# A graph network in one kernel: row loads of walk tables, the turn amid the products, scores ahead of the norm

## The reference

```python
edge_index = jnp.stack([src, dst])
h = jnp.maximum(_layernorm(x, axis=-1), 0.0)
x = x + _L0_gnn_ref(h, edge_index, ...)     # two SAGE convolutions, log softmax
h = jnp.maximum(_layernorm(x, axis=-1), 0.0)
x = x + _L1_gnn_ref(h, edge_index, ...)     # GAT, 4 heads of 128, batch norm, feed-forward
h = jnp.maximum(_layernorm(x, axis=-1), 0.0)
x = x + _L2_gnn_ref(h, edge_index, ...)     # GAT, 2 heads of 64, PReLU
h = jnp.maximum(_layernorm(x, axis=-1), 0.0)
x = x + _L3_gnn_ref(h, ..., src, dst, edge_type_4)  # max over edges, 4 relations
```

## Time and profile before

| | |
|---|---|
| three runs | 5915.43, 5924.08, 5924.83 us; median 5924.08 |
| the profiled execution | 5918.01 us, its span 5916.3 us |
| busy of the span | TensorE 3311.7 us (56%), VectorE 2935.2 (50%), ScalarE 1891.2 (32%), GpSimd 3914.0 (66%) |
| instructions | 100,213 |
| granted TensorE clock | 0.722 of full in the mean |

### The profile page before, as it was taken

One profiled execution on the slowest core, in us unless ns is written; L12 is line 12 of the kernel. 1 busy time (PEld: TensorE's weight loads), 2 busy tenths in 40 slices (PEclk: granted clock), 3 DMA queues, 4 the chain that ended last, 5 costly groups with the idle time before them and its releaser, 6 DMA issues. The chain is left out here.

```text
span 5916.3 us, 100213 instructions
## 1 busy us (share of the span) xinstructions
PE 3311.7 (56%) x15772; PEld 2786.6 (47%) x15773; DVE 2935.2 (50%) x7620; ACT 1891.2 (32%) x6493; POOL 3914.0 (66%) x4083
## 2 busy tenths in 40 slices
PE   3445555544565535889899894344555563333332
PEld 3444455444555524667777644233444533333331
DVE  4233344434455665788888744344555552222221
ACT  2111111111122204667777653233444441111110
POOL 4777777677777657777776005777777317777776
PEclk8666777766767757999999995566677785555555
DMA  4222222212122123444443211222222134444443
GB/s 122 61 62 63 64 65 66 71 52 53 52 53 53 48 47 87 109 115 116 115 111 106 99 38 38 54 53 53 53 53 53 25 105 131 131 130 132 133 131 108
DMA packets 441904, 474.75 MB, mean 80 GB/s; under 512 B 131954, under 2 KB 337214, under 8 KB 441695
## 3 DMA queue, kind: packets, MB, share of 16 engines
q0 software_dynamic: 130464, 264.37, 18.5%
q1 hardware_dynamic: 184116, 146.31, 8.2%
q10 hardware_dynamic: 127227, 63.09, 3.6%
HBM read 315.46 MB, written 157.97 MB: 80 GB/s over the span
## 5 line engine op out<-in xcount | busy, mean ns | idle before, releaser
L1175 PE MATMUL pa<-arena,weighted 128*128 x4480 | 871.3, 370 | 843.6 <-POOLq L893 510.2
L1175 PEld LDWEIGHTS pa<-arena,weighted 128*128 128x128 f32 x4480 | 803.8, 275 | 899.7 <-issue 899.4
L422 POOL DMA_INDIRECT arena<-y_tab,slot x784 | 739.7, 944 | 442.7 <-ACT slot L514 233.7
L1592 POOL DMA_INDIRECT arena<-t_tab,src_idx x784 | 788.1, 1005 | 283.2 <-issue 225.0
L899 POOL DMA_INDIRECT arena<-h_tab,src_idx x784 | 742.2, 947 | 307.3 <-issue 232.5
L2478 POOL DMA_INDIRECT arena<-t_tab,src_idx x784 | 751.1, 958 | 244.9 <-issue 232.5
L899 POOL DMA_INDIRECT arena<-sage_tab,src_idx x784 | 739.9, 944 | 261.3 <-issue 227.7
L471 DVE TENSOR_TENSOR_SCAN scan_t<-mask,scan_t,pa 128x512 f32<-128x512 bf16 x196 | 250.8, 1280 | 736.8 <-PE pa L495 736.8
L495 PE MATMUL pa<-ident,arena 128*128 128x128 f32 x784 | 218.5, 434 | 603.3 <-DMA arena<-y_tab,slot 603.3
L2716 PE MATMUL pa<-weighted 128*128 128x130 f32 x2240 | 440.2, 377 | 77.7 <-ACT weighted L2798 51.1
L495 PEld LDWEIGHTS pa<-ident,arena 128*128 128x128 f32 x784 | 140.4, 217 | 681.3 <-DMA arena<-y_tab,slot 428.2
(11 more groups left out here) (515 smaller groups left out, 6572.2 us busy)
## 6 DMA issues: line engine op xcount, KB each, us to landing
gat_tab<-out_rows SPq DMA_DIRECT2D x248, 260.0 KB
scan_rows<-out_rows ACTq DMA_DIRECT2D x196, 256.0 KB, 3.7
arena<-t_tab,src_idx POOLq DMA_INDIRECT x1568
mask<-cut_row SPq DMA_DIRECT2D x196, 128.0 KB, 3.1
arena<-h_tab,src_idx POOLq DMA_INDIRECT x784
arena<-sage_tab,src_idx POOLq DMA_INDIRECT x784
y_tab<-arena SPq DMA_DIRECT2D x49, 256.0 KB, 2.3
arena<-y_tab,slot POOLq DMA_INDIRECT x784, 2.8
```

The costliest lines, as they stand in the source:

```text
L422: nc.gpsimd.indirect_dma_start(out=rows(c, t), out_offset=None, in_=table[:, :], in_offset=bass.IndirectOffsetOnAxis(ap=slot[:, c, t:t + 1 ...
L1175: ins = nc.tensor.matmul(pa[:, b * CE:b * CE + RW], hot[b][:, t * P:(t + 1) * P], ring[:, bass.ds(start + t * RW, RW)], start=(t == 0), st ...
L1592: nc.gpsimd.indirect_dma_start(out=rows[:, g % QR * QT + t, :], out_offset=None, in_=t1_tab[:, :], in_offset=bass.IndirectOffsetOnAxis(ap= ...
```

## The change

A. `loaded_values` loads several values with one instruction and checks no bounds; `window_values` does it for a stretch of a window's row. The tables of a GAT are laid as one row for each window: 28 integers in `walk_rows1`, 24 in `walk_rows`. GAT1: ScalarE loads 16 registers (8 places in the ring, 8 offsets) and 10 registers (8 places, tile, groups needed) at the start of a window's body, VectorE 3 and 8. GAT2: ScalarE 8 at the start and 6 ahead of `stage_window`, VectorE 12 at the start and 3 ahead of `run`. In the walk passes TensorE's two loads for a step are one of two registers. `lay_walks` of GAT2 has four more copies and one more memset.

B. In `project` with `by_tile`, TensorE's turn and ScalarE's keep of group i+1 stand before the fifth tile of group i, not before its first, and the products of tiles go round four banks of PSUM instead of two.

C. In `project` with `starts`, VectorE waits for product i and does post i before front i+2.

```diff
+            banks = (pb[:, 0:CE], pb[:, CE:2 * CE], pd[:, 0:CE], pd[:, CE:2 * CE])
...
                     def step(i, b, left):
-                        if left > 1:
+                        if left > 1 and starts is None:
                             front(dve, i + 2)
                         dve.wait_ge(group_product.sem, group_product.past(i + 1))
                         post(dve, i, b)
+                        if left > 1 and starts is not None:
+                            front(dve, i + 2)
...
                         for t in range(NG):
                             if by_tile is not None:
+                                if t == 4 and left > 0:
+                                    turn(i + 1)
                                 ws, bias, n, _ = by_tile
 
-                                pe.wait_ge(tile_out.sem, tile_out.by_last_lap(i * NG + (t + 1 if t > 1 else 2 - t)))
-                                to = pb[:, t % 2 * CE:t % 2 * CE + n]
+                                pe.wait_ge(tile_out.sem, tile_out.by_last_lap(i * NG + (max(t, 1) if t < 3 else max(t - 1, 2))))
+                                to = banks[t % 4][:, 0:n]
...
-                        if left > 0:
+                        if left > 0 and by_tile is None:
                             turn(i + 1)
...
-                        if left > 0:
+                        if left > 0 and by_tile is None:
                             keep(i + 1, 1 - b)
                         if by_tile is not None:
                             for t in range(NG):
+                                if t == 4 and left > 0:
+                                    keep(i + 1, 1 - b)
                                 if t == NG - 2 and left > 1:
                                     scalar_front(act, i + 2)
                                 copy_product(i, t)
...
+        def loaded_values(kind, at, bounds):
+
+            why = "the walk tables are made on the chip from counts below these bounds"
+            _, values = nc.values_load_multi_w_load_instructions(at, engines=(kind,), skip_runtime_bounds_check_because=why)
+            return [nc.s_assert_within(value, low, high, skip_runtime_bounds_check_because=why)
+                    for value, (low, high) in zip(values, bounds)]
+
+        def window_values(kind, table, w, first, bounds):
+
+            last = first + len(bounds)
+            at = table[0:1, w, first:last] if isinstance(w, int) else table[0:1, bass.ds(w, 1), first:last].rearrange("o w k -> o (w k)")
+            return loaded_values(kind, at, bounds)
...
-                        start = pe.value_load(at[:, :, 0:1].rearrange("o s k -> o (s k)"), min_val=0, max_val=(RG - 1) * GT * RW)
-                        need = pe.value_load(at[:, :, 1:2].rearrange("o s k -> o (s k)"), min_val=1, max_val=GN)
+                        start, need = loaded_values(mybir.EngineType.PE, at.rearrange("o s k -> o (s k)"), [(0, (RG - 1) * GT * RW), (1, GN)])
...
-                        tile = of_fine(dve, w + 1, QW, 0, ET)
+                        tile, _, back = window_values(mybir.EngineType.DVE, walk_rows1, w + 1, 3 * QW, AHEAD1)
+                    if here:
+                        starts = window_values(mybir.EngineType.DVE, walk_rows1, w, 0, STEP1)
...
+                    if here:
+                        steps = window_values(mybir.EngineType.Activation, walk_rows1, w, 0, STEP1 + PLACE1)
+                    if next_here:
+                        *rows, tile, need = window_values(mybir.EngineType.Activation, walk_rows1, w + 1, 2 * QW, STEP1 + AHEAD1[0:2])
...
+                        values = window_values(mybir.EngineType.DVE, walk_rows, w, 0, STEP2 + PLACE2 + BLOCK2)
...
-                    need = of_walk(act, w, WT + 1, 1, GN)
-                    tile = of_walk(act, w, WT, 0, ET)
+                    *rows, tile, need = window_values(mybir.EngineType.Activation, walk_rows, w, 3 * WT, STEP2 + AHEAD2[0:2])
...
                     for k in range(WT):
-                        start = of_walk(act, w, k, 0, (RB - 1) * GT * BW)
...
                     if here:
-                        weigh(w, 0)
-                        weigh(w, 1)
+                        at = window_values(mybir.EngineType.Activation, walk_rows, w, 0, STEP2 + PLACE2)
+                        weigh(w, 0, at[0], at[WT])
+                        weigh(w, 1, at[1], at[WT + 1])
```

More of the change, by code:

```diff
@@ L1793, in run, with link @@
                                          run1[:, P - 1:P], ALU.add, ALU.max).then_inc(window_run.sem, 1)
-                def link(w, step, tile):
-                    back = of_fine(dve, w, QW + 2, 0, QK)
+                def link(w, step, tile, back):
                     v.tensor_copy(here1, tile_row1[:, :, bass.ds(tile, QK)])
@@ L1855, in body @@
                             if q == 4:
-                                link(w + 1, steps, tile)
+                                link(w + 1, steps, tile, back)
                             if q == 5:
@@ L1993, in _, with stage_flags @@
             def _(act):
-                def stage_flags(w):
-                    tile = of_fine(act, w, QW, 0, ET)
+                def stage_flags(w, tile, need):
                     after(act, window_scored, w)
@@ L2041, in body @@
                         if here:
-                            weigh(w, q, {t + 1: part for t, part in enumerate(beside)})
+                            weigh(w, q, steps[q], steps[QW + q], {t + 1: part for t, part in enumerate(beside)})
                         else:
@@ L2589, in run, with chain @@
                     v.tensor_tensor_scan(run_t, cut_t, own_row, -BIG, ALU.add, ALU.max).then_inc(window_run.sem, 1)
-                def chain(w, step, tile):
-                    back = of_walk(dve, w, WT + 2, 0, WK)
+                def chain(w, step, tile, back):
                     v.tensor_copy(tile_here, tile_row[:, :, bass.ds(tile, WK)])
```

130 lines of the change are left out of this document (61 added, 69 removed).

## The result

The changed kernel takes 5881.92 us in the median of four runs (5876.16 to 5883.32), the kernel before 5924.45; the ratio is 0.9927, with a 95% interval from 0.9916 to 0.9939. The profiled execution took 5876.16 us, its span is 5874.4 against 5916.3: 41.9 less. The forecast was 27.4 less on that span and 5893 for the median.

A forecast was written before the change was run, and what follows sets the result against it. GpSimd bounds the edge and walk passes and early windows; late GAT1 windows their own work, late GAT2 windows latencies. Terms 9.6 + 22 - 4 - 35 - 20 - 1 + 1 = -27.4 us on 5918.0 gave 5890.6, stated as 5893; range 5869 to 5907.

The forecast's parts named there:

- Project 1: First projection: scores before norm makes a 12.05 us chain per group, against 9.64 of scatter; +9.6 us, +8 to +11.
- Project 2: Second projection, norm on ScalarE: one chain of 14.4 us per group against 9.3; +22 us, range +17 to +25.
- The 80 in its list of signs: Expected sign in the second projection: scatters end 80 us after their first start instead of 65.
- the turn amid the products alone would be good: Second projection: this move alone helps, since the turn no longer waits for the norm ahead of all products; no size given.
- The rival that the two overlap in an unseen way: Projections lose nothing, since product and norm overlap in a way not seen; kernel at some 5853 us; chance 0.05.
- Project 3: Third projection: the first tile's product can start earlier, and half of the 8 us counts; -4 us, 0 to -8.
- Price of a read: Sequencer's row reads: 0.28 us for one register and 0.05 for each further one, 1.0 us for 16.
- rival A: Row reads: each register is its own trip; some 5960 us at 0.2 us each, 6015 at 0.275; chance 0.28.
- GAT1: Twenty late windows limited by their own work: 32.5 us each instead of 33.7; -20 us, range -10 to -30.
- GAT2: Late windows, a loop of latencies: 21.0 us each instead of 23.1 with fewer load delays; -35 us, -29 to -40.

The follow-up runs named there:

- projections alone: Kernel before with only the projections' edits (turn amid the products, four banks, scores ahead of the norm), all loads as before: 5952.24 us, ratio 1.0041.
- norm-first kernel: Changed kernel with the norm ahead of the scores again, turn amid the products and four banks kept: 5857.77 us, ratio 0.9881.
- row loads alone: Kernel before with the row loads, the function `project` as before: 5856.02 us, ratio 0.9880.
- The square above: Four kernels, reads single or in rows, checked or not; ratios to the kernel before (single, checked): single unchecked 0.9908, rows unchecked 0.9880, rows checked 1.0080.
- the moved reads: Kernel with the row loads alone, four reads moved behind work that might hide them: 7472.44 us (ratio 0.9699) and 7496.94 (0.9677), on slower chips.

## Why the prediction was right, point by point

**Project 1** held: +9.6 forecast, +8.9 here and +10.5 in the projections alone; copies 12.36 apart for 12.05. The copy, the product and the norm stand in one chain, and GpSimd waits 3.4 us a group where 2.4 were forecast: the seven scatters of a group take 9.0 us by themselves, and the 9.64 of the prediction was a mean in which the first three groups of before took 10.0 to 11.2.

**Project 2** held in its mechanism, every link with its size (7.8, 2.5, 0.9, 2.8, 0.3); 14.11 for 14.4 a group, GpSimd's wait of 5.4 as written. The 22 us became 18.3 because the scatters took 87.6 us from first to last, where the sum implies some 90 (first copy at 3588.7, scatter 0.9 behind it, end near 3680), and began 4.0 us sooner instead of 3. The 80 in its list of signs doesn't follow from its own sum. The norm-first kernel, which begins as early, shows that the sooner start comes from the turn amid the products. The prediction's remark that the turn amid the products alone would be good did not come true: it brings nothing in project 2's length (345.4 against 346.3). The rival that the two overlap in an unseen way (chance 0.05) is refuted by the projections alone.

**Project 3**: the step that failed is that half of the earlier start reaches the end. The start is 7 to 10 us earlier, the end isn't: 127.7 before, 127.4 with these edits alone, 127.7 with row loads and norm first. The 3.1 us less of the changed kernel are there in the row loads alone too (124.9) and are no larger than what this stage varies by with the same code (124.9 to 128.3), so the -4 is neither shown nor missed by its number.

**Price of a read** held where it carried the sum: 1.0, 0.8 and 0.6 us were taken for 16, 12 and 8 registers, 1.03, 0.85 and 0.56 are measured. For 10 (0.7 taken, 1.40 measured in most windows and 1.00 without other engines' reads beside it), 6 (0.5, 0.76), 3 and 2 it was too low. A single load has one assertion (L2451 has 240 of them for 240 reads) where the prediction counts two checks. So rival A, a trip for each register, is refuted, and with it what the Trainium skill's page "Runtime: NRT & Kernel Launch" (section "Instruction fetch mechanics") would give here: at its 200 ns per register sixteen would be 3.2 us, an estimate, and the trace has 1.03. The page speaks of loads from HBM; for a table in SBUF the trace disagrees for sixteen, and a read of two lies near 0.27 a register.

**GAT1**: the mechanism was right where it was priced. The prediction took the gain from the last twenty windows, 32.5 us each at their own pace and -20 in all; they have a median of 32.4, and together they are 21 us shorter. The other 9 of the 29.8 came before them, in the first ten windows, where the prediction had nothing. In the row loads alone the two parts are 22 and 2, with the norm first 18 and 4, so that this second part varies between kernels whose GAT1 differs by one check a row at most, and no run shows its cause.

**GAT2**: -35 forecast, -38.8 measured; the start of a window 0.5 us earlier on ScalarE and 0.9 on VectorE, where 0.6 was forecast for each, and the four staging copies within 0.52, where 0.25 apart was forecast. Of the 38.8, 32 came in the last twenty windows and 6 before them. The median window is 20.6 for 21.0, but the mean of the twenty is 21.5, because some still wait for gathers. So the near hit of the sum is in part luck: a little less than forecast in the windows that were priced, and a little more in those that were not.

**What the sum didn't say** is which part of a load cost the time. The prediction named both the checks and the reads and priced them as one. The square above shows that they don't simply add. Without the checks single loads already gain 54 of the 70 us and have the late windows of unchecked rows, and merging the reads brings the other 17. With the checks kept, merging the reads costs time (0.8% on its chip): there the checks stand together at the window's start. The sum came out right because the change does both; the sentence "the change makes one read per row and drops the checks" should have been two terms.

The whole: -27.4 forecast, -41.9 measured, and the difference is GAT1 (10), GAT2 (5) and project 2 (4), less what the walk passes vary (3) and a few tenths.

## What to carry to other kernels

Where one engine makes the next input and also takes the last product, taking first turns an overlap into a chain: here 12.4 us a group instead of 9.6, and 14.1 instead of 9.3, for a first scatter that came 2.4 us sooner in project 1. Of register loads, drop the bounds checks that stand behind a wait before you merge the reads: unchecked single loads had three quarters of the gain, and merged reads that kept their checks were slower than the single ones. And a load that is moved should go behind long work on its own engine, not behind a wait that has just ended: that is what the timeline of the moved reads shows.

## What the runs showed of the hardware

A check of a loaded value costs about 0.21 us of ScalarE's sequencer (one register operation of 147 ns and an assertion of 18 ns; 183 and 23 on VectorE), beside a read of one register from SBUF of 280 ns (309 on VectorE). These come from the rows with every value checked and from the kernel before.

A read of several registers doesn't cost by their number: 0.54 us for two, 0.56 for eight, 0.76 for six, 0.85 for twelve, 1.03 for sixteen, 1.40 for ten, on different engines and from different places in a row. On VectorE in GAT1 three registers take 0.77 and eight 0.60. The ten take 1.35 to 1.53 when reads of SyncE and VectorE begin within them and 1.00 when none does, in the changed kernel and in the row loads alone. That the other reads are the cause was not tested, and what else sets the price was not found.

On three of the four chips of the experiments the engines other than GpSimd paused between instructions while gathers were issued: activations 1.4 us apart instead of 0.25, and a kernel of 7,637 to 7,736 us instead of 5,926. The row loads gained more there (3.0% against 1.2%), and the projections' order was worth less than can be told. The number of instructions alone isn't the reason: the rows with every value checked have fewer than the kernel before and were slower. Whether it is the supply of instructions or something else on those chips, no run here shows.
